# Least of a row's four negated maxima in the second cross-attention: by two GpSimd operations on scalars in place of one VectorE operation

## The reference, cut to what matters

```
def _fq_unsigned(x, axis):
    s = jnp.max(x, axis=axis, keepdims=True) / 255.0
    s = jnp.maximum(s, 1e-08)
    q = jnp.clip(jnp.round(x / s), 0.0, 255.0) * s
    return x + jax.lax.stop_gradient(q - x)
...
attn = jnp.einsum('bhqd,bhkd->bhqk', q, k)
attn = jax.nn.softmax(attn.astype(jnp.float32), axis=-1)
attn = _fq_unsigned(attn, axis=-1)
out = jnp.einsum('bhqk,bhkd->bhqd', attn, v)
```

## Time and profile before

| | |
|---|---|
| median of 3 runs | 683.85 us |
| the profiled execution | 682.87 us, its span 681.1 us |
| TensorE busy in the span | 587.4 us (86%) |
| VectorE busy | 493.7 us (72%) |
| ScalarE busy | 401.7 us (59%) |
| GpSimd busy | 335.9 us (49%) |
| mean granted TensorE clock | 0.92 of full speed |

### The profile page before, as it was taken

The page is one execution under the profiler, slowest core; times in us unless marked ns, Lnnn a source line. Parts: engine busy times, 40 slices in busy tenths (PEclk is TensorE's granted clock), DMA queues, the critical chain, the costliest instruction groups (busy, mean ns, idle before and its releaser), DMA issues. The chain is left out here.

```text
span 681.1 us, 12859 instructions
## 1 busy us (share of the span) xinstructions
PE 587.4 (86%) x4813; PEld 398.3 (58%) x4813; DVE 493.7 (72%) x846; ACT 401.7 (59%) x754; POOL 335.9 (49%) x265
## 2 busy tenths in 40 slices
PE   4976899997899999788964988988888878889997
PEld 3542354444677776567740565655555465668886
DVE  4357999996677874567776999999999955433322
ACT  4226975552535544457875999999999953421111
POOL 1009999996204443243615889888888840000000
PEclk9987999999999999999975787779879869999999
DMA  8626600000936664035566889896979738900000
GB/s 336 254 74 252 247 0 1 0 1 0 303 119 212 211 218 130 16 115 147 150 167 149 162 129 183 152 168 136 165 159 149 132 64 326 408 2 1 0 1 15
DMA packets 97091, 92.90 MB, mean 136 GB/s; under 512 B 70596, under 2 KB 88324, under 8 KB 93639
## 3 DMA queue, kind: packets, MB, share of 16 engines
q1 hardware_dynamic: 84352, 85.74, 46.3%
q10 hardware_dynamic: 12678, 6.36, 3.2%
HBM read 68.59 MB, written 6.62 MB: 110 GB/s over the span
## 5 line engine op out<-in xcount | busy, mean ns | idle before, releaser
L2133 DVE TENSOR_REDUCE d_nmax<-d_psum 128x1 f32<-128x1024 f32 x128 | 152.0, 1214 | 6.0 <-PE d_psum L2289 6.0
L2289 PE MATMUL d_psum<-kst,qT 96*128 96x512 bf16 x256 | 97.2, 479 | 32.8 <-ACT d_e L2230 13.6
L528 POOL TENSOR_TENSOR b_h<-b_h,b_cb 128x1024 f32<-128x1024 f32 x32 | 88.0, 2750 | 6.5 <-DVE b_h L578 5.7
L2230 ACT ACTIVATE d_e<-d_psum,d_nmax 128x1024 f32<-128x1024 f32 x64 | 71.3, 1118 | 14.5 <-DVE d_nmax L2133 14.0
L2113 POOL TENSOR_SCALAR d_rounded<-d_e,d_lift 128x1024 f16<-128x1024 f32 x64 | 72.8, 1137 | 13.0 <-issue 7.0
L2113 POOL TENSOR_SCALAR d_rounded<-spare,d_lift 128x1024 f16<-128x1024 f32 x62 | 70.2, 1133 | 16.9 <-ACT d_lift L2234 12.6
L578 DVE TENSOR_TENSOR_SCAN b_h<-b_dA,b_psum 128x1024 f32<-128x1024 f32 x32 | 73.1, 2286 | 2.5 <-ACT b_dA L633 2.0
L633 ACT ACTIVATE b_dA<-b_dtT,b_A 128x248 f32<-128x248 f32 x128 | 53.7, 490 | 33.1 <-DVE b_h L578 28.1
L2230 ACT ACTIVATE spare<-d_psum,d_nmax 128x1024 f32<-128x1024 f32 x64 | 71.4, 1121 | 1.9 <-DVE d_nmax L2133 1.9
L2316 PEld LDWEIGHTS d_psum<-d_ident_f,d_rounded 128*128 128x128 f16 x512 | 44.1, 120 | 32.8 <-issue 20.9
L689 PE MATMUL b_psum<-b_bdiag,b_dtx 128*128 128x512 f32 x128 | 60.2, 594 | 0.8 <-DVE b_h L578 0.8
(11 more groups left out here) (439 smaller groups left out, 1185.5 us busy)
## 6 DMA issues: line engine op xcount, KB each, us to landing
c_w<-in_w0gu SPq DMA_DIRECT2D x16, 768.0 KB, 4.8
kst<-kT_scratch SPq DMA_DIRECT2D x84, 128.0 KB, 2.7
w<-in_w SPq DMA_DIRECT2D x5, 1920.0 KB, 21.0
b_cb<-c_scratch SPq DMA_DIRECT2D x4, 2048.0 KB, 6.9
c_w<-in_w0dn SPq DMA_DIRECT2D x16, 384.0 KB, 5.7
kT_scratch<-k_kT ACTq DMA_DIRECT2D x15, 384.0 KB, 2.7
a_ctx<-in_ctx SPq DMA_DIRECT2D x2, 2048.0 KB, 19.8
k_ctxT<-in_ctxT SPq DMA_DIRECT2D x12, 256.0 KB, 3.0
```

Source lines behind the costliest of these rows:

```text
L528: nc.gpsimd.tensor_tensor(hv, hv, cv, ALU.mult).then_inc(hc_ready, 1)
L2133: nc.vector.tensor_reduce(nm[:, t, m:m + 1, f:f + 1], quarter(m, j).unsqueeze(1), AX.X, ALU.max, negate=True).then_inc(nm_ready, 1)
L2230: nc.scalar.activation(e[j].unsqueeze(1), quarter(m, j).unsqueeze(1), ACT.Exp, bias=nm[:, t, m:m + 1, f], accum_out=zp[:, t, m:m + 1, f]). ...
L2289: last = nc.tensor.matmul(quarter(m, j)[:, b * 512:(b + 1) * 512], qT[0:QROWS, m:m + 1, t * P:(t + 1) * P], kst[m % 2][0:QROWS, at:at + 51 ...
```

## The change

GpSimd takes over the line that finds `mb`. One VectorE operation over the four columns of a block (an addition of log 255, and a running minimum into `mb`) goes. In its place GpSimd runs two operations on one column each. The first takes the least of the first three negated maxima into `least`. The second waits for the first, takes the least of that and the fourth, and adds log 255. They stand in GpSimd's list ahead of the block's four roundings.

```
-        raised = sb("d_nmax_raised", [P, QT])
+        least = sb("d_nmax_least", [P, 1])
...
+        least_ready = sem("d_least_ready")
...
+                def least_of(m, t):
+                    pool.wait_ge(nm_ready, m * APH + (t + 1) * QT)
+                    nc.gpsimd.tensor_scalar(least[:, :], nm[:, t, m, 0:1], nm[:, t, m, 1:2], nm[:, t, m, 2:3], ALU.min,
+                                            ALU.min).then_inc(least_ready, 1)
+                    pool.wait_ge(least_ready, m * TC + t + 1)
+                    nc.gpsimd.tensor_scalar(mb[:, t, m, QT - 1:QT], least[:, :], nm[:, t, m, 3:4], LOG255, ALU.min,
+                                            ALU.add).then_inc(mb_ready, 1)
...
+                        if f == 0:
+                            least_of(m, t)
                         pool.wait_ge(lift_ready, m * TC + (t + 1))
...
-                    if f == QT - 1:
-                        dve.wait_ge(nm_ready, m * APH + (j + 1))
-                        nc.vector.tensor_scalar(raised[:, :], nm[:, t, m, :], LOG255, NEG, ALU.add, ALU.min,
-                                                accum_out=mb[:, t, m, QT - 1:QT]).then_inc(mb_ready, 1)
```

## The result

The changed kernel takes 714.37 us (median of 4 runs, 713.65 to 716.13), the kernel before 683.56 us in the same comparison (4 runs, 681.04 to 685.11). The ratio on record is 1.042, with a 95% interval of 1.038 to 1.046: slower by some 29 us.

What follows compares the result with a forecast made beforehand. VectorE was taken to set the pace; the change closes a ScalarE-GpSimd loop of 13.56 us per head against 11.80. That adds 24.7 us over 14 heads plus 2.4 at the start, 27.1 in all: median 711 us, range 705 to 718.

Steps and rivals of the forecast that it cites:

- What bounds the kernel: Steady part, 400 to 548 us: VectorE, busy 144.3 of 148 us, sets the pace of 11.80 us per head.
- the rival of 677 us: VectorE stays the bound and the freed 6.7 us all come back, if GpSimd is free by the first lift; chance 0.05.
- The sum: Whole kernel: 24.7 us over 14 heads plus 2.4 us at the start, 27.1 us more than before.
- What the change removes: On VectorE, line 2137 costs 0.21 us each time, 6.7 us for 32 of them.
- What it adds: On GpSimd, 64 one-column operations, two in each of 32 blocks, priced from other operations in the trace.
- X: Time from GpSimd being free to `mb` written, two operations and the handover between them: 0.55 us.
- The outer end of 0.9: Upper limit in us kept for GpSimd's pair with its handover, since the operand form was unknown.
- The loop: ScalarE and GpSimd wait on each other from first lift to first lift: 13.56 us per head against 11.80.
- The second lift isn't delayed by its own pair: Within a head, GpSimd's second pair is done 5.8 us after the first lift, before ScalarE arrives at 6.41.
- The start: Head 0, behind the all-reduce: the pair waits for GpSimd's late first operation, putting head 1's first lift 2.4 us later.
- What would show it: Signs in the changed profile: ScalarE idle about 1.8 us before first lifts, VectorE's share about 84%, head 0's lift near 365.8.
- TensorE as a rival: A low TensorE clock slows quarters 4 to 7, adding up to 0.4 us per head, 717 us; chance 0.10.

Runs made afterwards that it cites:

- the kernel with a third operation: The changed kernel plus a third one-column GpSimd operation between the two of each pair, which waits for the first: 728.95 us, ratio 1.0609 to the kernel before.
- the first block only: Against the changed kernel, GpSimd runs the pair for each head's first block only, VectorE finds `mb` for the second: 711.93 us, ratio 1.0387 to the kernel before.
- the pair ahead of the scaling: Against the changed kernel, the first block's pair stands before GpSimd's scaling of the values, not behind it: 711.03 us, ratio 1.0376 to the kernel before.
- ahead of the last rounding: Pair on GpSimd for first blocks only, moved before the previous head's last rounding: 695.12 us, against 711.93 with the pair in the old place.

## Why the prediction was right, point by point

- *What bounds the kernel* was only half right. VectorE is the fullest engine, but not alone at the bound: with its operation gone, 0.09 us per head came back, not 0.42, and with the keys' loads moved as well 0.3 us. By the runs without the operation, the rival of 677 us could not have come true even with GpSimd at no cost. The sum does not rest on this reading, since it takes the 11.80 us as measured. The step that failed is the reading of the earlier trace rows alone. A share of 97% says that an engine has little slack, not that others have more. I did not look at the waits of TensorE, where the wait for keys stood.
- *What the change removes*, 0.21 us each, was right as a spacing, and worth nothing.
- *What it adds*: X, taken as 0.55 us, is 0.75, the term of the sum that was furthest off: the first operation lasts 0.36 us, the second starts 0.46 us after it and lasts 0.29. Both are far above MEMSET, and the first is above the 0.29 us that I had as the dearest. The outer end of 0.9 held. The Trainium skill's rule that a GpSimd instruction is to be timed by the spacing of starts (Perfetto Trace Analysis, § GPSIMD Engine Instruction) would have had me count two spacings, 0.50 us. The rows of the kernel with a third operation agree with the rule: a row of 0.36 us pushes the next start back by 0.46.
- *The loop* was right. Term by term: first to second lift 6.37 (6.41), second lift to roundings 0.41 (0.39), roundings 4.84 (4.82), scaling to the pair 1.24 (1.36), X 0.75 (0.55), handover 0.04 (0.03). The sum is 13.65 against 13.56. That it is so close is partly luck: X came out 0.20 us too small, and the pair starts 0.12 us sooner behind the scaling than a rounding does.
- *The second lift isn't delayed by its own pair*: right in the changed kernel, as the first block only shows. What I missed is that this holds only under the longer loop. I did not sum up GpSimd's own round, so I did not see that the pair on the second block alone costs 0.44 us per head, and that the work without any wait of ScalarE makes rounds of 12.7 us, half of the way to 13.65.
- *The start*: 2.4 us forecast, 2.8 measured from the start of the stage, within the 0.8 us by which that step varies.
- *The sum*: 27.1 us forecast. From the start of the stage on the two profiles differ by 28.9 us (31.5 less the 2.6 ahead of it), the medians by 30.8. 711 us against 714.4, in the range of 705 to 718. The missing 3.4 us are X and the start (some 1.7 us), and the rest is within what executions of one kernel differ by.
- *What would show it*: ScalarE's wait at first lifts is 1.3 and 1.8 us in turn, and once 0.3 (1.8 forecast), VectorE's share 84.6% (84%), the first lift of head 0 at 368.2, and 2.6 of that is the later stage (365.8).
- *TensorE as a rival*: its clock fell, but first lift to second lift took 6.37 us at 0.69 and at 0.63, none of the 0.4 us of the rival, so TensorE stays outside the loop.

## What to carry to other kernels

Before an operation is moved to a less busy engine, look at what stands in front of it in that engine's list at the moment when its result is wanted, and add up the chain through the engine that waits. Pairs of 0.75 us cost 1.85 us per head: some 0.9 as work in GpSimd's round, and as much again because they closed a loop over two in-order engines. Then sum the round of the engine that takes the work: idle time of 0.9 us doesn't hold 0.75 us of work if its result must come back through another engine first. And before counting on the relief of a full engine, leave its operation out altogether and see how much time that gives.

## What the runs showed of the hardware that I had not expected

- A GpSimd TENSOR_SCALAR on 128 rows of one column with three operands per row lasts 0.36 us, and 0.29 us with two and a constant. One that depends on it starts 0.46 us after its start. On VectorE the one operation over four columns that they replace cost 0.21 us.
- GpSimd's four roundings of a first block and VectorE's rounding of the values (lines 2158 to 2172, by kernel) overlap in time, and either one or the other is longer then. Four profiles (the kernels before and after, and those with the pair ahead of the scaling and ahead of the last rounding) have 56 such groups between 380 and 560 us. In 25 of them VectorE's instruction lasts 0.41 to 0.46 us and the group 4.91 to 5.15. In the other 31 VectorE's lasts 0.55 to 1.32 us and the group 4.75 to 4.81. One of the first kind, inside the row of 5.00 us of the kernel with the pair ahead of the scaling, and one of the second kind, inside the row at 465.29 of the changed kernel:

```profile
451.19 0.42 DVE L2166 TENSOR_SCALAR d_vh<-d_vh_scaled 128x512 f16<-128x512 f32 x1
...
468.12 0.98 DVE L2165 TENSOR_SCALAR d_vh<-d_vh_scaled 128x512 f16<-128x512 f32 x1
```

The two kinds go with the two lengths of heads of the kernel with the pair ahead of the scaling (13.32 and 13.12 us). No run varied the meeting by itself, so that the two engines hold each other up is a reading of these rows and not shown by an experiment.
- TensorE's mean granted clock from 400 to 548 us fell from 0.83 to 0.68 when the loop got longer, and the time of the loop did not notice: with 32 matmuls per head less it was 0.63, at the same 13.65 us.
